# The last stage of a two-layer attention and expert kernel: four of sixteen adds on GpSimd

## The reference, cut to what matters

```python
x = x + _L1_ffn_ref(_layernorm(x, axis=-1), L1_ffn_router_w, ...)
...
    routing_weights, routing_idx = jax.lax.top_k(probs, TOP_K)      # TOP_K = 2
    ...
    return jnp.einsum('bted,bte->btd', expert_out, expert_w)
```

## Time and profile before

| | |
|---|---|
| runs of the kernel before | 837.39, 839.63, 841.24 us |
| median | 839.63 us |
| the profiled execution's own time | 841.21 us |
| its span in the trace | 839.2 us |
| TensorE, VectorE, ScalarE, GpSimd busy | 77%, 52%, 51%, 43% of the span |
| last scatter issued on GpSimd, first add, last add of the last stage | 817.56, 823.55, 834.03 us |

### The profile page before, as it was taken

How to read it: one execution, slowest core, us unless ns; L and a number is a source line. 1 busy time by engine, 2 the same in 40 slices (tenths; PEclk the granted TensorE clock), 3 DMA queues, 4 the chain that set the end, 5 groups by cost and what they waited for, 6 DMA issues and landing times.

```text
span 839.2 us, 22056 instructions
## 1 busy us (share of the span) xinstructions
PE 647.6 (77%) x7845; PEld 462.8 (55%) x7845; DVE 439.7 (52%) x1179; ACT 424.8 (51%) x1044; POOL 356.8 (43%) x555
## 2 busy tenths in 40 slices
PE   1574549899996799896599888887713999999980
PEld 1352337676774445453366666665511887887860
DVE  1362356576772375754467886888551222222215
ACT  0683426576775234443156665666511666666650
POOL 4483340000000243533144476777871455545550
PEclk9996768899999799998589998999855999999995
DMA  3389832454401964786314343400111122222108
GB/s 87 116 228 182 209 125 50 74 107 79 79 2 21 196 209 180 204 248 261 144 37 91 67 85 74 100 25 25 34 48 51 52 56 58 65 58 56 55 29 303
DMA packets 59705, 87.52 MB, mean 104 GB/s; under 512 B 8904, under 2 KB 50128, under 8 KB 56528
## 3 DMA queue, kind: packets, MB, share of 16 engines
q1 hardware_dynamic: 51024, 75.03, 34.8%
q0 software_dynamic: 4352, 8.99, 3.4%
q10 hardware_dynamic: 4224, 2.10, 0.8%
HBM read 43.99 MB, written 41.96 MB: 102 GB/s over the span
## 4 chain that ended last, share of the span: by engine, by line
PE 29%; DVE 8%; POOL 4%; issue 4%; ACT 2%; DMA 2%; SPq 1%; POOLq 0%; ACTq 0%; DVEq 0%
PE bank L1526 6%; PE bank L1509 6%; PE bank L1512 5%; DVE nm L892 4%; PE bank L1519 3%; POOL sorted_in L1091 2%; PE bank L648 1%; ACT pr L795 1%; DMA kk<-results 1%; POOL pr L1061 1%; PE bank L686 1%; PE bank L740 1%; PE bank L704 1%; PE bank L1501 1%; PE bank L665 1%
## 5 line engine op out<-in xcount | busy, mean ns | idle before, releaser
L795 ACT ACTIVATE pr<-bank 128x512 f32<-128x512 f32 x256 | 147.1, 603 | 80.2 <-PE bank L689 77.6
L892 DVE TENSOR_REDUCE nm<-bank 128x8 f32<-128x1024 f32 x128 | 155.8, 1222 | 51.1 <-PE bank L665 49.1
L1606 DVE TENSOR_TENSOR exac<-bank,exsi 128x352 f32<-128x352 f32 x72 | 37.8, 524 | 125.4 <-PE bank L1512 123.2
L1061 POOL TENSOR_SCALAR_AFFINE_SELECT pr<-pr 128x1024 f32<-128x1024 f32 x64 | 69.8, 1091 | 66.6 <-ACT pr L795 66.1
L704 PE MATMUL bank<-pr,values 128*9 128x128 f32 x2048 | 83.7, 283 | 3.9 <-POOL pr L1061 2.0
L1487 POOL DMA_INDIRECT results<-exy,exre x72 | 71.0, 985 | 33.8 <-issue 33.8
L686 PE MATMUL bank<-qq,kk 48*128 48x128 bf16 x1024 | 77.5, 224 | 7.5 <-issue 3.7
L689 PE MATMUL bank<-mt,pick 64*128 64x128 bf16 x1024 | 77.4, 224 | 1.9 <-issue 1.9
L1336 PE MATMUL bank<-e0ch,expert_w 128*128 128x512 f32 x128 | 70.8, 635 | 6.5 <-DVE e0ch L1258 6.5
L1091 POOL DMA_INDIRECT sorted_in<-rrrow,rrpli x64 | 63.4, 990 | 14.2 <-issue 14.2
L1526 PEld LDWEIGHTS bank<-down_w,exat 128*128 128x128 f32 (+1 forms) x432 | 59.1, 191 | 17.0 <-issue 4.3
(11 more groups left out here) (212 smaller groups left out, 1282.9 us busy)
## 6 DMA issues: line engine op xcount, KB each, us to landing
sorted_in<-values SPq DMA_DIRECT2D x25, 715.0 KB, 6.5
k_parts<-pj_parts SPq DMA_DIRECT2D x16, 384.0 KB, 3.8
kk<-k_parts SPq DMA_DIRECT2D x32, 192.0 KB
qq<-q_parts SPq DMA_DIRECT2D x32, 192.0 KB
exx<-sorted_in SPq DMA_DIRECT2D x72, 65.0 KB
kk<-k_parts SPq DMA_DIRECT2D x32, 128.0 KB
qq<-q_parts SPq DMA_DIRECT2D x32, 128.0 KB
q_parts<-pj_parts SPq DMA_DIRECT2D x8, 384.0 KB, 3.6
```

Of the source, the lines that this page charges most:

```text
L795: act.activation(probs[c], st_bank[(n * NC + c) % ST][:], ACT.Exp, scale=scale).then_inc(exp_s, 1)
L892: dve.tensor_reduce(neg_max[n % 2][:, u * 2 * C4:(u + 1) * 2 * C4], score_banks(n, u).rearrange("q (h k) -> q h k", k=T), AX_X, ALU.max, n ...
L1061: pool.affine_select(out=probs_pair[u][:], in_=probs_pair[u][:], compare_op=ALU.is_ge, fill=0.0, base=0, pattern=[[0, 2 * C4], [1, T]], ch ...
```

## The change

In the groups with an odd number (1, 3, 5 and 7) GpSimd makes the first of the two adds. It waits for the group's load and counts the add on a new semaphore, `begun_s`. VectorE then waits for that count and makes the second add. In the even groups VectorE makes both, as before. Loads, stores and their order stay as they are.

```diff
             def on_vector(dve):
                 for n in range(NG):
                     x = x_res[:, n * G:(n + 1) * G, :]
-                    dve.wait_ge(y_in[n], 16)
-                    dve.tensor_tensor(x, x, y_g[n][:, :, 0, :], ALU.add).then_inc(first_s, 1)
-                    dve.wait_ge(first_s, n + 1)
+                    if n % 2:
+                        dve.wait_ge(begun_s, n // 2 + 1)
+                    else:
+                        dve.wait_ge(y_in[n], 16)
+                        dve.tensor_tensor(x, x, y_g[n][:, :, 0, :], ALU.add).then_inc(first_s, 1)
+                        dve.wait_ge(first_s, n // 2 + 1)
                     dve.tensor_tensor(x, x, y_g[n][:, :, 1, :], ALU.add).then_inc(sum_s, 1)
 
-            return Stage(on_sync, None, on_scalar, on_vector, None)
+            def on_gpsimd(pool):
+                for n in range(1, NG, 2):
+                    x = x_res[:, n * G:(n + 1) * G, :]
+                    pool.wait_ge(y_in[n], 16)
+                    pool.tensor_tensor(x, x, y_g[n][:, :, 0, :], ALU.add).then_inc(begun_s, 1)
+
+            return Stage(on_sync, None, on_scalar, on_vector, on_gpsimd)
...
                     causal.gpsimd(pool)
                     experts.gpsimd(pool)
+                    total.gpsimd(pool)
```

More of the change, by code:

```diff
@@ L1636, in combine @@
             y_in, first_s, sum_s, x_out = [s(f"y_in{n}") for n in range(NG)], s("first"), s("sum"), s("x_out")
+            begun_s = s("begun")
             by_token = results[0:SPARE].rearrange("(t c) d -> t (c d)", t=T)
```

## The result

The changed kernel is slower by 0.42%: the ratio of its 20 runs to 20 of the kernel before is 1.0042, with a 95% interval from 1.0023 to 1.0062 (medians 840.93 and 837.44 us; single runs spread over 12 us after and 9.5 us before). On 837.44 that is +3.5 us, between 1.9 and 5.2. The forecast was +3.1 us, to 842.7 us. Its base was the median of three runs, 839.63 us; that of the twenty is 2.2 us lower, so the measured median lies 1.8 us under the forecast one, while the two differences are 0.4 us apart.

What follows compares the result with a forecast made beforehand. The loads' last landing and the stores' volume were taken to bound the last stage. GpSimd's late drain moves its end from 839.2 to 842.3: 839.63 + 3.1 = 842.7 us, range 839.3 to 845.0.

Steps and rivals of the forecast that it cites:

- The bound of the stage: Last stage: loads, last landing at 833.3, and store volume bound it; four adds (2.8 us) off VectorE buy nothing.
- The drain: Block's end: GpSimd's DRAIN takes 6.6 us of its own behind GpSimd's last add, ending at 842.1; span +3.1 us.
- The waiting between the engines: Last stage's adds with SBUF operands run one after another, 13.4 us in all; last sum at 836.9, +2.2 us.
- The store path: Stage's end: last store issued 2.2 us later, 0.8 us hidden by queue; +1.2 us, hidden under the drain.
- the first rival: Block's end: drain's part belongs to the last scatter, ends at 825.8, costs nothing; stores decide, +1.2 us, 840.8; chance 0.26.
- Tied to the last scatter: Same as the first rival: drain ends at 825.8 as before, total 840.8 us; chance 0.26.
- The whole 8.47 us are the drain's own: Block's end: the drain runs its full 8.47 us after the last add; +5.0 us, 844.6; chance 0.12.
- Neither drain nor waiting: Last stage: adds run side by side, last sum 0.6 us late, hidden by store queue; 839.6 us; chance 0.08.

Runs made afterwards that it cites:

- the kernel with groups 1, 3 and 5: Changed kernel with GpSimd adding in groups 1, 3 and 5 only, VectorE making both adds of group 7; last stage 19.5 us long.
- the kernel with GpSimd's adds beside: Kernel before, all sixteen adds on VectorE, plus one unneeded 128x512 GpSimd add per group for which nobody waits; last stage 25.6 us.
- the kernel with the early drain: Changed kernel plus one GpSimd DRAIN between last scatter and GpSimd's first add; ratio 1.0013 to the kernel before, stage 20.1 us.
- the tiny instruction: Kernel before, all adds on VectorE, plus a one-column GpSimd multiplication after the last group's load; stage 21.7 us.

## Why the prediction was right, point by point

*The bound of the stage* held. The loads' end did not move with VectorE's work (the last add that waits for a load starts 13.5 us after the first load's issue, 13.4 before), the DMA share stayed over 1 until the loads were in, and the store queue hid late sums. One sign that the prediction gave did not come: the DMA share was to drop below 0.9 between 834 and 838 if the sums were late. They were late, and it was 1.15 there, and 1.15 too from 835.3 to 839.3, the same piece of the stage after.

*The drain* is the whole effect, as forecast. Its own part behind the last add was 7.28 us. I had taken the middle of 5.95 and 7.26, because I did not know whether it counts from the scatter's recorded end or from its landing; it was the upper end, the work itself, done over the indirect DMAs since the last drain. GpSimd's last add ended 14.8 us behind the first load's issue (836.0 - 821.22); I had put 835.5 - 819.90 = 15.6. The two errors, +0.7 and -0.8, cancelled: 22.3 us of stage, 22.4 forecast.

*The waiting between the engines* was right in kind and too dear in size. I summed twelve VectorE adds and four GpSimd adds without overlap, 13.4 us; the run had 837.2 - 825.2 = 12.0 us. With 0.67 us for a VectorE add and 1.0 for a GpSimd add beside it the same sum is 12 x 0.67 + 4 x 1.0 = 12.0. The 1.0 is a mean: for the first of the four VectorE stood idle for 1.21 us, waiting for the count, and the others cost it less. In the kernel with groups 1, 3 and 5 it comes out again, 838.4 - 826.75 = 11.7 us for 13 x 0.67 + 3 x 1.0.

*The store path* was mis-sized: +1.2 us forecast, 0.1 measured. One half is the sums, 1.1 us late and not 2.2. The other is the queue's share of the last store's 4.0 us. I estimated a fresh store of 256 KB at 3.2 us from loads and stores of 384 KB. In the kernel with GpSimd's adds beside, the last sum ended at 843.2, and the store was in at 845.6, at a DMA share of 0.57 in between. So one with little queue takes 2.4 us, and some 1.6 us can hide. The kernel with the early drain agrees about: sums 2.1 us late, stores 0.8 us late. It did not matter while the drain ended later, but it would have put the first rival at about 0 instead of +1.2 us.

*The rivals.* "Tied to the last scatter" is out by the tiny instruction and by the drain moved forward. "The whole 8.47 us are the drain's own" is out: the record starts when the sequencer reaches the drain, and the own part starts behind the last work. "Neither drain nor waiting" is out by both.

*What was not settled.* By the length of its stage no version here is faster than the kernel before. The best with GpSimd's help are level with it (stages of 19.4 and 19.5 us against 19.3), because the stage belongs to the DMA engines.

## What to carry to other kernels

Work on GpSimd at the end of a block in which it has issued indirect DMAs is not free, even when GpSimd is idle there: its drain then stands behind that work. Look in the rows by line for the DRAIN of each engine and ask what hides it. If GpSimd must work late, drain it once before, beside something else. And before moving a VectorE add to GpSimd, see whether both read their operands from SBUF: beside each other such adds take turns, and here the moved add cost VectorE 1.0 us where it saved 0.67.

## What the runs showed of the hardware that I had not expected

- GpSimd's DRAIN takes 0.083 us for each indirect DMA (of 128 rows) since the last drain, from 32 to 104 of them (2.70 us at 32, 8.56 us at 104), and 7.25 to 7.28 us with 120 or 136. All had long landed where adds stood in front of the drain, and it was 7.28 us all the same.
- The 114th indirect DMA since a drain has 1.3 to 1.7 us of issue in front of it where most scatters have 0.45.
- A GpSimd multiplication of one column, 0.18 us elsewhere, took 0.69 us when it started during a VectorE add of two SBUF operands, and ended 0.05 us behind it.
- A fill of 128x512 float32 on GpSimd took 0.52 us in this stage, an add of the same shape 1.26.
